# Image stores moved to ScalarE's queue, mixing weights paced on GpSimd's queue, in a Fourier layer network with a token tail

## The chip, the cores and the metric

One core of a Trainium2 chip runs the kernel. The metric is the device time of one execution in microseconds.

## What is computed

64 images of 64 x 64 pixels with 3 channels go through four Fourier layers of width 32 and a small MLP; what comes out is one value per pixel. That map of 64 rows of 64 values for each image then goes through attention, two mixture-of-experts layers and a recurrent layer. The change touches the first part alone:

```python
h = layer_norm(x @ fc0_w + fc0_b, ln0_g, ln0_b)          # (64, 64, 64, 32)
for i in range(4):
    # 12 x 12 modes at the low and high end of the spectrum, mixed over channels
    x_ft = rfft2(h);  out_ft[..., :12, :12] = einsum('bixy,ioxy->boxy', x_ft[..., :12, :12], w1[i])
    out_ft[..., -12:, :12] = einsum('bixy,ioxy->boxy', x_ft[..., -12:, :12], w2[i])
    h = irfft2(out_ft) + einsum('bchw,oc->bohw', h, conv_w[i]) + conv_b[i]
    h = layer_norm(h, ln_g[i], ln_b[i])
    if i < 3: h = gelu(h)
h = gelu(h @ fc1_w + fc1_b); h = gelu(h @ fc2_w + fc2_b); h = h @ fc3_w + fc3_b
```

All is float32. The real and imaginary parts of `w1` and `w2` are four inputs (`w1r`, `w1i`, `w2r`, `w2i`) of 4 layers x 32 x 32 x 144 values.

## The kernel before

**Groups and phases.** The 64 images are worked through in 16 groups of four. The image state h is 2 MB a group and lives in HBM (`h_scratch`); the spectrum stays on the chip. Phase `first` makes h from x and transforms it (16 groups). Phase `mid` runs three times (L = 0 to 2): for each group it transforms the mixed spectrum back (`i1` and the second half of `acc`), adds the convolution of h (`acc`), normalises, applies gelu and transforms the new h forward (`f1`, `f2`). Phase `last` does the fourth layer's inverse transform and the MLP. After it comes the token part, which the change doesn't touch.

**Bodies.** The work is software-pipelined by a string per engine (`ORDER`, from L141). A body `b` does the early steps of group b and the late ones (marked with a minus) of group b - 1. In the mid phase ScalarE's string is `gelu.2- back.1- acc.0 sq.0 gelu.3- back.2- acc.1 sq.1 back.3- acc.2 sq.2 gelu.0 acc.3 sq.3 pack.0- gelu.1 back.0 pack.1-`, and TensorE's begins `i1.0 turn.2- back.1- acc.0 i1.1`. In the first phase ScalarE has `xt.0 gelu.2- back.1- acc.0 back.2- sq.0 gelu.3- acc.1 sq.1 back.3- acc.2 sq.2 gelu.0 ...`. The number behind a step is one of four quarters of the group: `acc.n` on ScalarE (L1441) copies the product pA into `raw`, `sq` (L1451) squares it, `gelu.n` (L1462) writes quarter n of `h_new`, TensorE's `back.n` (L1318) transposes it and ScalarE's `back.n` (L1466) copies that to `h_rows`. `gelu.0` and `gelu.2` wait until the store of the group before has landed (`stored0`, `stored1`), since they overwrite it.

**Mixing.** A layer's spectrum is mixed (`mix`, L1177) in two halves of 32 images. Half 0 of the next layer is mixed ahead of the last body of a phase, half 1 between bodies 1 and 2 of the layer. The outcome y goes to HBM (`y_scratch`) by four stores of GpSimd (`y_store`, L1137), and comes back by group in eight small loads of SyncE (`load_y`, L988) into `y_in`, which `i1` reads (L1253). Groups 0 to 7 need half 0, groups 8 to 15 half 1. The weights of a layer lie in `w_sb` in two slots. VectorE centres them (`cen`, L1585 to L1589) in bodies 3 to 8 (slot 0) and 9 to 14 (slot 1); before the first of them it waits for all eight loads (`w_loaded`).

**Queues.** SyncE's queue holds, for each group g (`group`, L1067): wait for the last `i1` (or `xt`) of g, load y (or x) of g + 1, wait for `acc` 2 and load half 0 of h of g + 1, wait for `acc` 4 and load half 1, then wait for quarters 2 and 4 of `h_new` of g and store the halves. Ahead of group 2 of each mid layer it waits for the y store of half 1 (`y_is_stored`). GpSimd's queue holds the eight weight loads of layer 0 at the very start, then per layer: y store of half 0, a copy of the convolution matrix, y store of half 1, and right behind it the eight weight loads of the next layer (`weights`, L1129). At the start SyncE loads the constants, x of group 0, 16 copies of fc0's weights and its bias row (L979, L980), then 16 small tables of `gam` and `bet` (L984, L985), which `gelu.0` of group 0 waits for.

Of the kernel before, what the change touches and what calls it, by code (L numbers as in the profile page):

```python
# [33 lines left out]
LAYERS = 4  # L34
# [181 lines left out]
def build(nc, ins, out_ap, B):  # L216
    NG = B // GI
# [17 lines left out]
    with ctx:  # L235
# [77 lines left out]
        def param(rows, cols):  # L313
# [43 lines left out]
        halves = lambda t: [t[:, 0:512], t[:, 512:1024]]  # L357
        SLOTS = {"d": [pD[:]], "s": [pS[:]], "a": [pA[:]], "r": halves(pT)}
        names = ["d_full", "d_free", "s_full", "s_free", "a_full", "a_free", "r_full", "r_free", "acc_full", "conv_ready", "copied", "squared", "summed", "rooted", "root_chain",
                 "turned", "h_new_ok", "x_loaded", "y_loaded", "y_clear", "packed", "h_loaded0", "h_loaded1", "stored0", "stored1", "fc0_clear", "y_stored", "w_loaded",  # L360
                 "w_centred", "mix_a_full", "mix_a_free", "mix_b_full", "mix_b_free", "y_bias", "conv_cleared", "conv_loaded", "conv_turned", "conv_chain", "cst_loaded", "ln_loaded",
                 "fc0_loaded", "fc0_chain", "mlp_cleared", "mlp_loaded", "normed", "eps_set"]
        names += ["td_full", "td_free", "ts_full", "ts_free", "par_cleared", "par_loaded", "tok_ready", "v_chain", "shifted",
# [466 lines left out]
        def alone(eng):  # L830

            eng.sem_inc(s["passed"], 1)
# [137 lines left out]
        def _(sp):  # L970
# [29 lines left out]
                c = slice(2048 * t, 2048 * t + 2048)  # L1000
                sp.dma_start(h_in[:, c], h_dram[g][:, c]).then_inc(s[f"h_loaded{t}"], 16)

            def store_h(ph, L, g, t):
                c = slice(2048 * t, 2048 * t + 2048)
                sp.wait_ge(s["h_new_ok"], at("h_new", ph, L, g, 2 * t + 2))
                sp.dma_start(h_dram[g][:, c], h_new[:, c]).then_inc(s[f"stored{t}"], 16)

            def conv_params():
                for j in range(4):
                    sp.dma_start(conv_rows[32 * j:32 * j + 32, :].rearrange("p (l c) -> p l c", l=LAYERS),  # L1010
# [56 lines left out]
            def group(ph, L, g, then=None):  # L1067

                p = Phase(ph, L)
                end = isinstance(g, int) and g == NG - 1  # L1070
                op = "xt" if ph == "first" else "i1"
                if not (end and ph == "last"):
                    p.sent(sp, op, p.ends(op)[1], g)
                if end and ph != "last":
                    y_is_stored(L if ph == "first" else L + 1, 0)
                    load_y(0)
                    for t in range(2):
                        sp.wait_ge(s[f"stored{t}"], at("stored", ph, L, g, 0) + 16)
                        alone(sp)
                elif not end:  # L1080
                    load_x(g + 1) if ph == "first" else load_y(g + 1)
                if ph == "first" and end or ph == "mid" or ph == "last" and not end:
                    for t in range(2):
                        if ph == "last":
                            p.sent(sp, "acc", 2 * t + 1, g)
                        elif ph == "mid":
                            sp.wait_ge(s["acc_full"], at("acc", ph, L, g, 2 * t + 2))
                        load_h(0 if end else g + 1, t)
                if then:
                    then()  # L1090
                if ph != "last":
                    store_h(ph, L, g, 0)
                    store_h(ph, L, g, 1)

            def groups(ph, L):

                group(ph, L, 1)
                if ph == "mid":
                    y_is_stored(L, 1)
                else:  # L1100
                    mlp_params()
                with sp.Fori(2, NG - 1) as g:
                    group(ph, L, g)
                group(ph, L, NG - 1)

# [19 lines left out]
        def _(pool):  # L1125
            pool.memset(arena[:, 7744:8384], 0.0).then_inc(s["conv_cleared"], 1)
            pool.memset(mlp, 0.0).then_inc(s["mlp_cleared"], 1)

            def weights(L):  # L1129
                for slot in range(2):  # L1130
                    for w, (wr, wi) in enumerate((("L0_tok_w1r", "L0_tok_w1i"), ("L0_tok_w2r", "L0_tok_w2i"))):
                        for r in range(2):
                            q = slice(64 * w + 32 * r, 64 * w + 32 * r + 32)
                            pool.dma_start(w_v[q, slot].rearrange("p o m -> p (o m)"),
                                           ins[wr if slot == r else wi][L].rearrange("i o x y -> i (o x y)")).then_inc(s["w_loaded"], 16)

            def y_store(L, half):  # L1137

# [8 lines left out]
                        src = w_sb[q:q + 32, 13312:17920].rearrange("b (w n) -> b w n", w=2)  # L1147
                        pool.dma_start(dst, src).then_inc(s["y_stored"], 16)

            weights(0)  # L1150
            for L in range(LAYERS):
                y_store(L, 0)
                if L == 0:
                    pool.wait_ge(s["conv_chain"], 2)
                else:
                    pool.wait_ge(s["acc_full"], at("acc", "mid", L, 0, 0))
                pool.tensor_copy(conv_bd[:], conv_all[:, P * L:P * L + P]).then_inc(s["conv_ready"], 1)
                y_store(L, 1)
                if L < LAYERS - 1:
                    weights(L + 1)  # L1160
            pool.wait_ge(s["mix_a_full"], 6 * LAYERS)
            pool.wait_ge(s["mix_b_full"], 6 * LAYERS)
            pool.memset(spec[:, 0:at_col[0]], 0.0).then_inc(s["par_cleared"], 1)
# [242 lines left out]
        def _(act):  # L1406
# [18 lines left out]
            def steps(p):  # L1425
# [39 lines left out]
                def back(n, g):  # L1465
                    act.copy(hrow_v[:, :, 512 * n:512 * n + 512],  # L1466
                             take("back", n, g).rearrange("p (t n) -> p t n", t=2)).then_inc(s["s_free"], 1)

                def pack(b, g):

# [39 lines left out]
        def _(dve):  # L1510
# [64 lines left out]
            def cen(n, g):  # L1575
# [1 line left out]
                L, i, part = centring["L"], centring["i"], centring["part"]  # L1577
                w = w_v[:, part, :, bass.ds(24 * i, 24)]
                first = 18 * part + n
                if n == 0 and part == 0:  # L1580
                    dve.wait_ge(s["w_loaded"], 128 * L + 128)
                dve.wait_ge(s["w_centred"], 36 * L + first + 1 + 3 * i)
                alone(dve)
                if n == 0:
# [95 lines left out]
```

## Time and profile before

| what | value |
|---|---|
| median of 3 runs | 3339.99 us (3336.26 to 3341.17) |
| the profiled execution | 3339.68 us |
| its span | 3337.9 us |
| TensorE busy | 2942.9 us, 88% |
| VectorE busy | 2146.3 us, 64% |
| ScalarE busy | 1948.7 us, 58% |
| GpSimd busy | 61.5 us, 2% |
| DMA | 335.90 MB, mean 101 GB/s |
| chain that ended last, by engine | TensorE 75%, VectorE 11%, issue 5%, ScalarE 5%, DMA 4% |

The first phase runs to about 430 us, the three mid layers to about 1915, the last phase to about 2680, the token part to the end. The chain is TensorE's in the main; the 4% of DMA in it are what is left for transfers to cost. A wait of an engine is printed with what ended it, and where its entry says "issue" the profile shows nothing that it waited for.

### The profile page before, as it was taken

The numbers are of one execution on the slowest core, as the hardware profiler recorded it, in microseconds if no ns is written. First come the engines' busy times: TensorE is split into PE (matmuls) and PEld (weight loads), VectorE is DVE, ScalarE is ACT, GpSimd is POOL, SyncE is SP. The second block draws the span as 40 slices with busy tenths as digits, with TensorE's granted clock in tenths as the row PEclk, the third lists the DMA queues.
The fourth block names the chain that finished last, engine by engine and source line by source line (L and its number), as shares of the span: only waits on it lengthen the run. The fifth ranks groups of instructions, "written<-read, shape, count | busy, mean of one in ns | idle before, by whom it ended". The sixth has DMA issues, their size and how long they took to land.

```text
span 3337.9 us, 82078 instructions
## 1 busy us (share of the span) xinstructions
PE 2942.9 (88%) x32240; PEld 1869.3 (56%) x32240; DVE 2146.3 (64%) x3954; ACT 1948.7 (58%) x2271; POOL 61.5 (2%) x81
## 2 busy tenths in 40 slices
PE   5888888999888999888999879999999987973994
PEld 2454555666555666565666644444444447962893
DVE  5888676888666888666888745444544444246457
ACT  4777655666545666455666547777777763422451
POOL 0000000000000000000000010000000001000000
PEclk9999999999999999999999999999999998986897
DMA  4222346444437444447444524111111000000000
GB/s 107 99 95 98 99 161 205 163 163 162 154 135 207 162 162 162 151 144 210 163 162 162 163 75 101 55 46 44 57 54 57 29 1 1 1 1 0 1 1 13
DMA packets 98092, 335.90 MB, mean 101 GB/s; under 512 B 29928, under 2 KB 61960, under 8 KB 62088
## 3 DMA queue, kind: packets, MB, share of 16 engines
q1 hardware_dynamic: 93832, 295.73, 25.7%
q0 software_dynamic: 4096, 37.75, 4.9%
q8 instruction: 131, 2.15, 0.3%
q14 instruction: 33, 0.27, 0.0%
HBM read 179.29 MB, written 154.14 MB: 100 GB/s over the span
## 4 chain that ended last, share of the span: by engine, by line
PE 75%; DVE 11%; issue 5%; ACT 5%; DMA 4%; SPq 0%; DVEq 0%; POOL 0%; ACTq 0%; POOLq 0%
PE pA L1281 14%; PE pA L1289 7%; PE pT L1375 7%; PE pS L1318 4%; PE pT L1307 4%; PE pD L1364 4%; PE pD L1332 4%; PE pD L1346 4%; PE pD L467 3%; PE pA L467 3%; PE pA L1271 3%; PE pD L1253 2%; DMA y_in<-y_scratch 2%; PE pS L459 2%; PE pT L459 2%
## 5 line engine op out<-in xcount | busy, mean ns | idle before, releaser
L1610 DVE TENSOR_REDUCE small<-arena 128x32 f32<-128x1056 f32 x320 | 396.8, 1240 | 322.5 <-ACT arena L1451 314.0
L1281 PEld LDWEIGHTS pA<-conv_bd,h_in 128*128 128x128 f32 x4096 | 479.8, 193 | 109.4 <-issue 92.7
L1281 PE MATMUL pA<-conv_bd,h_in 128*128 128x128 f32 x4096 | 518.1, 280 | 8.6 <-DVE arena L1603 2.9
L1441 ACT COPY w_sb<-pA 128x1024 f32<-128x1024 f32 x256 | 259.7, 1015 | 417.3 <-PE pA L1289 346.4
L1624 DVE SCALAR_TENSOR_TENSOR w_sb<-w_sb,small 128x1024 f32<-128x1024 f32 x320 | 386.6, 1212 | 5.5
L1462 ACT ACTIVATE h_new<-pT,bet,gam 128x1024 f32<-128x1024 f32 x256 | 307.4, 1201 | 126.6 <-PE pT L1307 121.1
L1451 ACT ACTIVATE arena<-w_sb 128x1024 f32<-128x1024 f32 x320 | 339.2, 1060 | 13.4
L1307 PEld LDWEIGHTS pT<-cst,w_sb 128*128 128x128 f32 x2048 | 225.5, 143 | 142.8 <-issue 124.4
L1307 PE MATMUL pT<-cst,w_sb 128*128 128x128 f32 x2048 | 283.3, 282 | 21.4 <-DVE w_sb L1624 21.1
L1466 ACT COPY h_rows<-pS 128x1024 f32<-128x1024 f32 x256 | 257.0, 1004 | 72.2 <-PE pS L1318 72.1
L1318 PEld LDWEIGHTS pS<-cst,h_new 128*128 128x128 f32 x2048 | 229.4, 143 | 113.4 <-issue 72.8
L1318 PE MATMUL pS<-cst,h_new 128*128 128x128 f32 x2048 | 276.6, 279 | 9.6 <-ACT h_new L1462 9.6
L1289 PE MATMUL pA<-arena,cst 64*64 64x512 f32 x2048 | 279.1, 615 | 1.7 <-DVE arena L1603 1.7
L1375 PE MATMUL pT<-w_sb,arena 128*64 128x512 f32 x1024 | 270.3, 616 | 2.9 <-ACT w_sb L1486 1.5
L1346 PE MATMUL pD<-arena,cst 64*32 64x384 f32 (+1 forms) x4096 | 208.2, 491 | 15.0 <-DVE arena L1643 9.9
L1486 ACT ACTIVATE w_sb<-pT,arena 128x512 f32<-128x512 f32 x256 | 173.1, 685 | 18.2 <-PE pT L1375 17.4
L1643 DVE STREAM_TRANSPOSE arena<-pD 128x768 f32<-128x768 f32 x128 | 125.4, 980 | 84.6 <-PE pD L1346 68.7
L1483 ACT ACTIVATE w_sb<-pD,arena 128x1024 f32<-128x1024 f32 x128 | 142.4, 1113 | 62.1 <-PE pD L1364 38.3
L1332 PE MATMUL pD<-h_rows,cst 64*32 64x512 f32 x2048 | 139.7, 600 | 36.5 <-DVE arena L1637 21.1
L1603 DVE STREAM_TRANSPOSE arena<-pD 128x1024 f32<-128x1024 f32 x96 | 119.8, 1248 | 74.9 <-PE pD L1253 74.2
L1637 DVE STREAM_TRANSPOSE arena<-pD 128x1024 f32<-128x1024 f32 x128 | 159.2, 1244 | 5.1 <-PE pD L1332 1.1
L1271 PE MATMUL pA<-arena 128*128 128x512 f32 x256 | 126.2, 617 | 27.1 <-DVE arena L1526 24.6
(299 smaller groups left out, 3921.2 us busy)
## 6 DMA issues: line engine op xcount, KB each, us to landing
h_scratch<-h_new SPq DMA_DIRECT2D x128, 1024.0 KB, 4.2
h_in<-h_scratch SPq DMA_DIRECT2D x128, 1024.0 KB, 5.0
y_scratch<-w_sb POOLq DMA_DIRECT2D x32, 576.0 KB, 8.4
y_in<-y_scratch SPq DMA_DIRECT2D x512, 36.0 KB
w_sb<-in_L_tok_w1r_dram POOLq DMA_DIRECT2D x8, 576.0 KB, 16.6
w_sb<-in_L_tok_w1i_dram POOLq DMA_DIRECT2D x8, 576.0 KB, 16.6
w_sb<-in_L_tok_w2r_dram POOLq DMA_DIRECT2D x8, 576.0 KB, 21.0
w_sb<-in_L_tok_w2i_dram POOLq DMA_DIRECT2D x8, 576.0 KB, 21.0
```

The lines of the kernel that those rows point to most:

```text
L1281: pe.matmul(pA[:, c:c + 128], h_in[:, 1024 * n + c:1024 * n + c + 128], conv_bd[:], start=(j == 0), stop=False, skip_group_check=True)
L1289: mm = pe.matmul(pA[64 * b:64 * b + 64, 512 * t:512 * t + 512].rearrange("p (x o) -> p o x", o=C), const["idft_y"][rows, 64 * b:64 * b + 6 ...
L1307: mm = pe.transpose(bank[:, 128 * j:128 * j + 128], raw[n][:, 128 * j:128 * j + 128], ident)
L1318: mm = pe.transpose(bank[:, 128 * j:128 * j + 128], h_new[:, 1024 * n + 128 * j:1024 * n + 128 * j + 128], ident)
L1332: mm = pe.matmul(out[q:q + 32, b], const["dft_y"][rows, NQ * b:NQ * b + NQ], src[rows, t, 32 * xh:32 * xh + 32, 16 * ch:16 * ch + 16], sta ...
L1346: mm = pe.matmul(out.rearrange("p (q h c) -> p h c q", h=2, c=16), const["dft_x"][rows, 128 * part + 32 * j:128 * part + 32 * j + 32], TA[ ...
L1375: mm = pe.matmul(bank[64 * j:64 * j + 64, :], fc2_w, G1[m % 2][:, 512 * j:512 * j + 512], start=True, stop=True)
L1441: act.copy(raw[n], pA[:]).then_inc(s["copied"], 1)
L1451: act.activation(sq[n % 2][:, :, 0:C], raw[n].rearrange("p (x o) -> p x o", o=C), ACT.Square, scale=float(C) ** -0.5).then_inc(s["squared" ...
L1462: act.activation(h_new[:, 1024 * n:1024 * n + 1024], pT[:], ACT.Gelu if ph == "mid" else ACT.Identity, bias=bet[:, col], scale=gam[:, col] ...
L1610: dve.reduce_sum(var[n], sq[n % 2], axis=AX).then_inc(s["summed"], 1)
L1624: dve.scalar_tensor_tensor(out=z, in0=z, scalar=ROOT_SCALE, in1=r.broadcast_to([P, 32, C]), op0=ALU.mult, op1=ALU.mult).then_inc(s["normed ...
```

## The change

Three things. (1) `store_h` is gone from SyncE: ScalarE issues the store of a half of `h_new` itself, right behind its copies `back.1` and `back.3`. (2) SyncE's wait for the y store of half 1 moves from ahead of group 2 to ahead of group 6; in the first phase the loads of the MLP's parameters move with it. (3) GpSimd issues the weights in pairs (`weights(L, slot, w)`), each behind a wait for a certain `acc` product: at the start in bodies 0, 1, 3 and 4; in a layer the first pair right behind the mix, the second behind `acc.1` of body 2, the y store of half 1 behind `acc.0` of body 4, and the pairs of slot 1 behind `acc.0` of bodies 5 and 6. VectorE waits per slot (`w_loaded0`, `w_loaded1`), with one more semaphore increment (`alone`) at each first step of the centring.

```diff
-            def store_h(ph, L, g, t):
-                c = slice(2048 * t, 2048 * t + 2048)
-                sp.wait_ge(s["h_new_ok"], at("h_new", ph, L, g, 2 * t + 2))
-                sp.dma_start(h_dram[g][:, c], h_new[:, c]).then_inc(s[f"stored{t}"], 16)
-
...
                 if then:
                     then()
-                if ph != "last":
-                    store_h(ph, L, g, 0)
-                    store_h(ph, L, g, 1)
 
             def groups(ph, L):
 
-                group(ph, L, 1)
+                with sp.Fori(1, 6) as g:
+                    group(ph, L, g)
                 if ph == "mid":
                     y_is_stored(L, 1)
                 else:
                     mlp_params()
-                with sp.Fori(2, NG - 1) as g:
+                with sp.Fori(6, NG - 1) as g:
                     group(ph, L, g)
                 group(ph, L, NG - 1)
...
+            def weights(L, slot, w):
+                wr, wi = (("L0_tok_w1r", "L0_tok_w1i"), ("L0_tok_w2r", "L0_tok_w2i"))[w]
+                for r in range(2):
+                    q = slice(64 * w + 32 * r, 64 * w + 32 * r + 32)
+                    pool.dma_start(w_v[q, slot].rearrange("p o m -> p (o m)"),
+                                   ins[wr if slot == r else wi][L].rearrange("i o x y -> i (o x y)")).then_inc(s[f"w_loaded{slot}"], 16)
+
+            def after(ph, L, g, n):
+
+                pool.wait_ge(s["acc_full"], at("acc", ph, L, g, n))
...
-            weights(0)
+            for slot in range(2):
+                for w in range(2):
+                    after("first", 0, 3 * slot + w, 1)
+                    weights(0, slot, w)
...
-                y_store(L, 1)
-                if L < LAYERS - 1:
-                    weights(L + 1)
+                if L == LAYERS - 1:
+                    y_store(L, 1)
+                else:
+                    n = 2 * L + 1
+                    pool.wait_ge(s["mix_a_free"], 3 * n + 3)
+                    pool.wait_ge(s["mix_b_free"], 3 * n + 3)
+                    weights(L + 1, 0, 0)
+                    after("mid", L, 2, 2)
+                    weights(L + 1, 0, 1)
+                    after("mid", L, 4, 1)
+                    y_store(L, 1)
+                    for w in range(2):
+                        after("mid", L, 5 + w, 1)
+                        weights(L + 1, 1, w)
...
                 def back(n, g):
                     act.copy(hrow_v[:, :, 512 * n:512 * n + 512],
                              take("back", n, g).rearrange("p (t n) -> p t n", t=2)).then_inc(s["s_free"], 1)
+                    if n % 2:
+                        c = slice(1024 * n - 1024, 1024 * n + 1024)
+                        act.dma_start(h_dram[g][:, c], h_new[:, c]).then_inc(s[f"stored{n // 2}"], 16)
...
-                if n == 0 and part == 0:
-                    dve.wait_ge(s["w_loaded"], 128 * L + 128)
+                if n == 0:
+                    dve.wait_ge(s[f"w_loaded{part}"], 64 * L + 64)
+                    alone(dve)
```

## Rows read from the trace of the kernel before

**Rows 1.** The waits of all engines: engine, line, tile, releaser: us in total, times, longest.
```profile
PE pD L1253 <- DMA y_in<-y_scratch: 27.1, 3, 10.7
```

**Rows 2.** The timeline, 0 to 60: start, us, engine, line, operation, idle time before.
```profile
10.87 0.25 SPq L980 DMA_DIRECT2D arena<-in_L_tok_fc_b_dram  x1
...
14.80 5.53 SPq L984 DMA_DIRECT2D gam<-in_L_tok_ln_g_dram  x1
...
28.87 0.42 DVE L1522 COPY arena<-arena 1x512 f32<-1x512 f32 x1 [23.10 <-DMA arena<-in_L_tok_fc_b_dram]
...
44.58 1.19 ACT L1462 ACTIVATE h_new<-pT,bet,gam 128x1024 f32<-128x1024 f32 x1
```

**Rows 3.** DMA issues by line: tile, count, size of each, median us to landing.
```profile
arena<-in_L_tok_fc_b_dram SPq DMA_DIRECT2D x2, 0.2 KB, 2.3
```

**Rows 4.** The timeline, 490 to 550: end of a mix and body 2 of L = 0.
```profile
505.23 0.50 POOL L1134 DMA_DIRECT2D w_sb<-in_L_tok_w1r_dram  x1
...
506.13 1.00 ACT L1466 COPY h_rows<-pS 128x1024 f32<-128x1024 f32 x1
...
508.47 0.91 PE L1253 MATMUL pD<-y_in,cst 48*32 48x208 f32 x32
...
514.15 1.01 ACT L1441 COPY w_sb<-pA 128x1024 f32<-128x1024 f32 x1 [1.44 <-PE pA L1289]
...
516.71 4.11 SPq L996 DMA_DIRECT2D y_in<-y_scratch  x8
...
520.55 1.21 ACT L1462 ACTIVATE h_new<-pT,bet,gam 128x1024 f32<-128x1024 f32 x1
...
541.41 1.59 PE L1253 MATMUL pD<-y_in,cst 48*32 48x208 f32 x32 [10.12 <-DMA y_in<-y_scratch]
...
546.94 1.45 DVE L1585 TENSOR_REDUCE small<-w_sb 128x24 f32 x1
```

**Rows 5.** Windows: us, busy PE, PEld, DVE, ACT, POOL, then clock, DMA share, GB/s.
```profile
531.30:541.40 10.10, 0.00 (x0) 0.02 (x1) 1.14 (x2) 1.34 (x2) 0.00 (x0) 0.64 1.01 221
```

**Rows 6.** TensorE's timeline from 560: `i1` of bodies 3 and 4, and two gaps.
```profile
572.12 0.91 PE L1253 MATMUL pD<-y_in,cst 48*32 48x208 f32 x32 [0.29 <-DVE arena L1643]
...
1026.87 1.57 PE L1346 MATMUL pD<-arena,cst 64*32 64x384 f32 x23 [1.30 <-issue]
...
1040.19 1.59 PE L1253 MATMUL pD<-y_in,cst 48*32 48x208 f32 x32 [10.72 <-DMA y_in<-y_scratch]
...
1070.68 0.91 PE L1253 MATMUL pD<-y_in,cst 48*32 48x208 f32 x32 [0.29 <-DVE arena L1643]
...
1098.33 0.91 PE L1253 MATMUL pD<-y_in,cst 48*32 48x208 f32 x32 [0.29 <-DVE arena L1643]
...
1528.35 0.85 PE L1346 MATMUL pD<-arena,cst 64*32 64x384 f32 x1 [3.60 <-issue]
...
1537.36 1.59 PE L1253 MATMUL pD<-y_in,cst 48*32 48x208 f32 x32 [6.26 <-DMA y_in<-y_scratch]
...
1566.77 0.91 PE L1253 MATMUL pD<-y_in,cst 48*32 48x208 f32 x32 [0.29 <-DVE arena L1643]
```

**Rows 7.** Line 1006, SyncE's stores of h_new: duration of the issue, and landing.
```profile
L1006 SPq DMA_DIRECT2D h_scratch<-h_new x128: 332/355/372, 49.8 to 1928.1; - x128
...
DMA to landing us min/median/max: 3.9/4.2/21.5
```

**Rows 8.** ScalarE's timeline, 560 to 590: a mid body.
```profile
577.80 1.02 ACT L1441 COPY w_sb<-pA 128x1024 f32<-128x1024 f32 x1 [1.35 <-PE pA L1289]
...
587.55 1.01 ACT L1441 COPY w_sb<-pA 128x1024 f32<-128x1024 f32 x1 [1.20 <-PE pA L1289]
```

**Rows 9.** ScalarE's timeline, 200 to 248: a body of the first phase.
```profile
223.58 1.01 ACT L1441 COPY w_sb<-pA 128x1024 f32<-128x1024 f32 x1 [0.32 <-PE pA L1271]
...
233.01 1.20 ACT L1462 ACTIVATE h_new<-pT,bet,gam 128x1024 f32<-128x1024 f32 x1 [0.36 <-PE pT L1307]
```

**Rows 10.** Line 1134, GpSimd's weight loads: landing.
```profile
DMA to landing us min/median/max: 7.3/20.7/35.7
```

More of the change, by code:

```diff
@@ L359, in build @@
         names = ["d_full", "d_free", "s_full", "s_free", "a_full", "a_free", "r_full", "r_free", "acc_full", "conv_ready", "copied", "squared", "summed", "rooted", "root_chain",
-                 "turned", "h_new_ok", "x_loaded", "y_loaded", "y_clear", "packed", "h_loaded0", "h_loaded1", "stored0", "stored1", "fc0_clear", "y_stored", "w_loaded",
+                 "turned", "h_new_ok", "x_loaded", "y_loaded", "y_clear", "packed", "h_loaded0", "h_loaded1", "stored0", "stored1", "fc0_clear", "y_stored", "w_loaded0", "w_loaded1",
                  "w_centred", "mix_a_full", "mix_a_free", "mix_b_full", "mix_b_free", "y_bias", "conv_cleared", "conv_loaded", "conv_turned", "conv_chain", "cst_loaded", "ln_loaded",
@@ L1127, in _ @@
             pool.memset(mlp, 0.0).then_inc(s["mlp_cleared"], 1)
[L1129 to L1135, printed above, removed]
+            def weights(L, slot, w):
[6 more added lines that the diff above has]
+                pool.wait_ge(s["acc_full"], at("acc", ph, L, g, n))
             def y_store(L, half):
```

## The prediction

> **What bounds the kernel now.** I read the waits first, sorted by total: they say which engine is stopped by a transfer, which is all that this change can touch. Of everything that TensorE waits for, one entry names a DMA: its L1253 (the inverse x transform, `i1`) waited 27.1 us in three goes for `y_in` [rows 1]. Then the timeline of the start. VectorE's copy of the fc0 bias row (L1522) starts at 28.87 after 23.10 us of idling for a load that SyncE had issued at 10.87 [rows 2]; a load of that size lands in 2.3 us elsewhere [rows 3]. What stands in its way are the eight mixing weight loads (576 KB each) that GpSimd issues in the first microseconds.
>
> Then the timeline of one layer (L = 0). The mix of half 1 is over at about 503. GpSimd stores y, and from 505.23 on issues the eight weight loads of the next layer [rows 4]. SyncE may load the y of group 3 only when that store has landed, so it issues it at 516.71 to 520.82, behind the weights, and it is in place at 541.4, 20.6 us later. TensorE has nothing from 531.3 on and starts at 541.41; in that gap its granted clock falls to 0.64 while the DMA engines are 1.01 busy [rows 4, 5]. In the other bodies of a layer TensorE goes from one `i1` to the next in 27.65 us (1070.68 to 1098.33) [rows 6] with waits of a few tenths; nothing there hangs on a DMA. So the gain, if any, lies at the start and once per layer, and the loss, if any, in the 60-odd ordinary bodies where ScalarE now issues stores.
>
> **The change part by part, against the profiled 3339.7 us (its span is 3337.9; the median of the runs, 3340.0, is the same number for my purpose).**
>
> *1. Start.* GpSimd's first weights now wait for the first `acc` product, which itself needs fc0. So nothing large is in flight when the fc0 row is issued at 10.87 (0.25 us). With 2.3 us to landing it is there at 13.4 [rows 3] instead of 28.87: 15.4 us earlier. All work after it moves with it, TensorE's slow first products too, since it idles before them either way. What is late next: `gelu.0`, at 44.58 [rows 2], would be at 29.2, and it needs the 16 small `gam`/`bet` loads that SyncE issues behind fc0. Without congestion these take 0.43 us each, and are issued by 18.7; one of them took 5.53 behind the weights [rows 2]. I take this as covered: **-15.4**, with 5 as the lower end if those loads are slow by themselves (issued by 27.5 as now, then landing at 39 instead of 29).
>
> *2. y of group 3.* The wait of SyncE for the half 1 store moves from ahead of group 2 to ahead of group 6, where the loads of group 7 on follow; the first group that reads half 1 is 8, so nothing reads too early. The store itself moves to the first `acc` of body 4 and has until body 6, over 40 us. The load of group 3's y now follows `i1.1` of body 2 (508.47 + 0.91 = 509.4), and its eight issues end near 514: 17.5 us ahead of its use at 531.3. It was 20.6 us from the last issue with eight weights, four y stores and four h transfers around it. Now half of the weights and no y stores are in that body. I take the wait as gone: **-27.1** [rows 1]. With the old 20.6 us, 3.1 us a layer would stay.
>
> *3. The body after the stall.* It starts at the low clock: 32 matmuls of `i1` take 1.59 us after the gap and 0.91 otherwise [rows 4, 6], and 1.59/0.91 is about the step between 2.4 and 1.2 GHz. Bodies 3 of the three layers take 30.71 (541.41 to 572.12), 30.49 and 29.41 us against 27.65 [rows 4, 6]: together 7.7 us over. With no gap this goes: **-7.7**.
>
> *4. Gaps put down to issue in body 2.* 1.30 us at 1026.87 and 3.60 us at 1528.35 [rows 6]: in the middle of a product, waiting for nothing, as if the engine's code came late. Such gaps are absent in the looped bodies. If the full DMA engines hold the code back they vanish (-4.9), if not, they stay (0). Half: **-2.5**.
>
> *5. Stores on ScalarE.* Two issues a body, 120-odd in all. On SyncE one takes 0.355 us, 0.372 at most, at any load of the DMA engines [rows 7], plus under 0.1 us for its address; no row shows a DMA issued by ScalarE. I take 0.45. Below it could be 0 (issue beside the running copy), above it GpSimd's 0.50 [rows 4] + 0.1. Behind `back.1` in the mid bodies ScalarE idles 1.35 us before `acc.0`, behind `back.3` 1.20 before `acc.2` [rows 8]: covered at either end, 0. In the first phase the idle time before `acc.0` is 0.32 [rows 9]; so `acc.0`, `sq.0`, `gelu.3` come 0.15 later, TensorE's `back.3` with them. Behind `back.3` there is next to nothing, but `gelu.0` has idled 0.36 before it [rows 9]. That leaves 0.1 to 0.3 a body, in 15 bodies at most 4.5: **+2**.
>
> *6. Where the stores are late.* `gelu.0` may overwrite `h_new` only when the store of half 0 has landed. Before, that was issued in the previous body. Now it is issued behind `back.1`: in body 2 after 507.1, ahead of `gelu.0` at 520.55 [rows 4], 13.4 us; in the first phase 223.7 to 233.0, 9.3 us [rows 9]. Landing is 4.2 us by the median, 21.5 at most [rows 7], and the long ones belong to the weight bursts. In bodies 1, 3 and 4 of the first phase two weight loads now start beside that store. Sharing the engines evenly doubles 4.2 to 8.4: just covered. **+1**, up to 9 (3 us in three bodies).
>
> *7. Weights in time?* The centring (`cen.0`, L1585) of body 3 stands 5.5 us behind its `i1` (546.94 against 541.41) [rows 4], so at 536.8 without the stall. It needs all four loads of slot 0; the last two are issued after `acc.1`, whose copy begins at 514.15 [rows 4], so by 515.2: 21.6 us. Landing took 7.3 / 20.7 / 35.7 us (least, median, most) with eight in flight [rows 10]. With two in flight I place it near the lower end. Slot 1 has bodies. By the longest landing VectorE would stand 14.1 us in each layer: bounds 0 and +42, taken **0**. The Trainium skill (DMA: Bandwidth & Descriptors, Anatomy of one DMA — SWDGE (gpsimd) path) gives such a transfer as about 2.0 us + bytes / 436e3, which is 3.4 us for one and under 7 for two. By that estimate this wait cannot occur; the rows, where the least is 7.3, are slower than it, and what stands above goes by them. The added `alone` and waits of VectorE at `cen` are 48 times under 0.05 us, **+0.5** in all counting that this engine is nearly full in the first phase.
>
> Sum: -15.4 - 27.1 - 7.7 - 2.5 + 2 + 1 + 0.5 = -49.2; 3339.7 - 49.2 = **3290 us**.
>
> **The rivals.**
> - *y still late.* y's small packets stand in SyncE's queue beside two others, ScalarE's stores and GpSimd's weights. For: DMA engines stay nearly full in body 2 (2.4 MB weights, 4.2 MB of h, 0.3 of y in 27.65 us are 248 GB/s, and 221 is what 1.01 gave [rows 5]). Against: the first two weights have 6 us of lead and are mostly in. Price: 3.1 us a layer, half of term 3 back (3.9) and term 4 (2.5): +15.7, 3306. The Trainium skill (DMA: Bandwidth & Descriptors, Queues, rings and completion order) says that each DMA engine takes turns between queues packet by packet; by that rule a third queue costs y a share of its turns, in the direction of this rival.
> - *The centring waits.* Landing of 27 us, between the median and the most of [rows 10], where 21.6 are free, gives 5.4 us of VectorE in three layers, +16 and 4 of clock: 3310.
> - *The start is bound by the small loads.* Term 1 is 5 instead of 15.4: 3300.
> - *ScalarE's issue is dear*, the one on the slower side. It sits ahead of `acc.0` and `acc.2` of every body. With c us per issue including its address, a mid body loses (c - 1.35) + (c - 1.20), a first body about (c - 0.68) + (c - 0.44). Over 48 and 15 bodies this is 50 us at c = 1.5: from there the change is a loss. At c = 1.8 it is 50 + 37 = 87 us: 3290 - 2 + 87 = 3375. For it: SyncE's one issue of 5.53 [rows 2] shows that an issue can block, and no row shows ScalarE's. Against: 128 large stores never took over 0.372 us [rows 7], even with full engines.
> - *It does not do what it says.* If the weights' bursts only move to other bodies and stall TensorE there, the 27.1 come back: bodies 5 and 6 get four loads together, where the stores' slack is 13.4 us and the y loads' 17. I hold this small: at most 20 us, 3310.
>
> **How the numbers follow.** The forecast has 0.68, with its own range of 3280 to 3300 (terms 4 and 5 at their ends, terms 6 and 7 partly). Late y 0.10, centring 0.06, small loads at the start 0.08, moved bursts 0.03, dear issue 0.05. The range of 8 in 10 is **3276 to 3314**: from all of term 4 and a free ScalarE issue, with some more of the clock, to the late y and centring cases together with first-phase store waits. A measurement of this kernel tells 0.2% (6.7 us) from no change. Faster by more than that: 0.94 (all cases but dear issue, less a little); within it: 0.02; slower: 0.04.
>
> **What the profile after would show.** Right: L1522 starts near 13 us; no wait of L1253 for `y_in`; bodies 2 and 3 of each layer at 27.65 to 29 us; ScalarE's issues at 0.3 to 0.5 us with mid bodies still at 27.65 and first bodies at most 0.3 longer; L1585 of body 3 not waiting for a weight load. Wrong: `gelu.0` or `gelu.2` (L1462) waiting for `h_scratch<-h_new`, above all in bodies 1, 3 and 4 of the first phase; L1585 or L1462 of group 0 waiting for a DMA; longer mid bodies. The prediction falls as a whole if ordinary bodies change by over half a microsecond, for there are 60 of them.

## The result, and the profile after

The changed kernel takes 3281.86 us (median of 4, 3278.74 to 3284.09) against 3338.55 beside it: ratio 0.983, 95% interval 0.981 to 0.985, 56.7 us faster. Forecast were 3290 and 49.2 us. Two of the nine executions of run 4 were far slower than the rest (3490 and 3808 us), and its time and ratio below leave them out. The profiled execution has a span of 3279.2 us, 58.7 less than before. Its page, the lines on busy time, the slices and the DMA queues, and from part 4 the chain by engine:

```profile
PE 2937.9 (90%) x32240; PEld 1867.7 (57%) x32240; DVE 2145.9 (65%) x3954; ACT 1950.3 (59%) x2271; POOL 61.9 (2%) x81
...
q1 hardware_dynamic: 75400, 161.50, 16.4%
q10 hardware_dynamic: 18432, 134.23, 10.0%
q0 software_dynamic: 4096, 37.75, 5.3%
...
PE 79%; DVE 11%; issue 5%; ACT 5%; DVEq 0%; SPq 0%; DMA 0%; ACTq 0%
```

The engines do the same work. ScalarE's stores are a queue of their own now (q10, 134 MB, what was taken off q1), and the DMA's part of the chain went from 4% to 0. The wait of TensorE for `y_in` [rows 1] is gone from the list of waits. The start, as in [rows 2] (timeline of all engines):

```profile
12.10 0.42 DVE L1535 COPY arena<-arena 1x512 f32<-1x512 f32 x1 [6.33 <-DMA arena<-in_L_tok_fc_b_dram]
...
14.07 3.75 PE L1281 MATMUL pA<-arena 128*128 128x512 f32 x4 [7.79 <-DVE arena L1539]
...
18.07 0.42 SPq L985 DMA_DIRECT2D bet<-in_L_tok_ln_b_dram  x1
18.13 0.67 POOL L1126 DMA_DIRECT2D w_sb<-in_L_tok_w1r_dram  x1 [16.49 <-PE pA L1281]
...
18.92 1.98 PE L1281 MATMUL pA<-arena 128*128 128x512 f32 x4 [1.10 <-ACT w_sb L1451]
```

The copy of the fc0 row starts 16.8 us earlier than in [rows 2], and all small tables are issued by 18.5 without one that blocks. Body 2 of L = 0 and the `i1` of bodies 3 and 4, as in [rows 4, 6] (TensorE's timeline; `i1` is L1263 here):

```profile
485.60 1.57 PE L1263 MATMUL pD<-y_in,cst 48*32 48x208 f32 x32 [1.24 <-ACT w_sb L1432]
...
513.26 1.58 PE L1356 MATMUL pD<-arena,cst 64*32 64x384 f32 x23 [0.48 <-issue]
...
516.01 0.91 PE L1263 MATMUL pD<-y_in,cst 48*32 48x208 f32 x32 [0.16 <-DVE arena L1657]
...
543.66 0.91 PE L1263 MATMUL pD<-y_in,cst 48*32 48x208 f32 x32 [0.29 <-DVE arena L1657]
```

In this layer body 2 begins at a low clock, behind the mix with its gaps on TensorE, as the stretches of the trace show (columns: stretch and its length; busy time and instructions of PE, PEld, DVE, ACT and POOL; granted clock; DMA share; GB/s):

```profile
485.60:489.00 3.40, 3.40 (x41) 2.75 (x42) 1.70 (x4) 0.00 (x0) 1.00 (x2) 0.52 0.74 173
489.90:492.00 2.10, 2.10 (x22) 1.93 (x24) 1.22 (x1) 1.44 (x2) 0.00 (x0) 1.00 1.00 202
```

A granted clock of 0.52 is near the 1.2 GHz level, and 1.00 follows within some 4 us. It is not so in every layer or execution: over its first 3.5 us body 2 has 1.00 in L = 1 and 0.59 in L = 2 of this trace, and 1.00 in L = 0 of a second one of the same kernel (run 9). The kernel before has 1.00, 1.00 and 0.54. There a low clock also came behind the late y, where now body 3 begins with a gap of 0.16 us and takes 0.91 us for its first product instead of 1.59:

```profile
541.40:543.00 1.60, 1.59 (x33) 0.81 (x34) 0.00 (x0) 0.00 (x0) 0.00 (x0) 0.50 0.98 385
```

(the kernel before, the same view, over that first product of body 3). Body 3 now lasts 27.65 us. GpSimd's part of bodies 2 to 4, then SyncE's, in their timelines:

```profile
485.80 0.50 POOL L1126 DMA_DIRECT2D w_sb<-in_L_tok_w1r_dram  x1 [95.60 <-ACT w_sb L1432]
...
498.70 0.49 POOL L1126 DMA_DIRECT2D w_sb<-in_L_tok_w2r_dram  x1 [11.90 <-PE pA L1299]
...
549.61 2.10 POOL L1144 DMA_DIRECT2D y_scratch<-w_sb  x4 [49.93 <-PE pA L1299]
```
```profile
493.94 4.23 SPq L996 DMA_DIRECT2D y_in<-y_scratch  x8
498.58 11.17 SPq L1001 DMA_DIRECT2D h_in<-h_scratch  x2
...
550.38 14.37 SPq L996 DMA_DIRECT2D y_in<-y_scratch  x8
```

In body 4, beside the four y stores of GpSimd, the eight y issues of SyncE take 14.4 us in place of 4.2 (14.0 and 14.4 in the other layers). Nothing waits for them: body 4 lasts 27.64 us.

And line 1480, ScalarE's stores, then line 1126, the weights, as in [rows 7, 10]:

```profile
L1480 ACTq DMA_DIRECT2D h_scratch<-h_new x128: 338/343/387, 34.4 to 1871.9; - x128
...
  ACT h_new L1472: 2.7, 1
...
DMA to landing us min/median/max: 3.9/4.5/14.1
```
```profile
DMA to landing us min/median/max: 5.4/7.7/11.2
```

The weights land in 7.7 us by the median where it was 20.7, and no store takes over 14.1 where it was 21.5.

Where the 58.7 us are, read from the starts of `xt` and `i1` in TensorE's timeline, before against after:

| stretch | before, us | after, us | difference |
|---|---|---|---|
| up to the `xt` of body 1 | 48.77 | 30.58 | -18.2 |
| from there to the first `i1` of L = 0 | 380.64 | 381.54 | +0.9 |
| bodies 2 of the three layers | 38.49 + 40.19 + 40.50 | 30.41 + 27.68 + 29.23 | -31.9 |
| bodies 3 of the three layers | 30.71 + 30.49 + 29.41 | 27.65 + 27.64 + 27.64 | -7.7 |
| all the rest | | | -1.8 |

The ordinary bodies of the layers are the same to 0.01 us (27.64), and twelve bodies of the first phase take 289.47 against 289.36. The figures of body 2 hold a part that changes between executions: the low clock at its start and gaps put down to issue are worth up to 3 us (30.41 and 27.51 us, both in L = 0 of the changed kernel).

### The profile page after: what moved, and what is told of

It reads as the page before. It is cut to its first block, busy times and chain, and to the rows that moved or that the text cites. A ratio compares the mean times of both kernels' runs of the same rounds, so it can differ in the third digit from the quotient of the medians.

```text
span 3279.2 us, 82177 instructions
## 1 busy us (share of the span) xinstructions
PE 2937.9 (90%) x32240; PEld 1867.7 (57%) x32240; DVE 2145.9 (65%) x3954; ACT 1950.3 (59%) x2271; POOL 61.9 (2%) x81
## 4 chain that ended last, share of the span: by engine, by line
PE 79%; DVE 11%; issue 5%; ACT 5%; DVEq 0%; SPq 0%; DMA 0%; ACTq 0%
PE pA L1291 15%; PE pA L1299 8%; PE pT L1385 8%; PE pT L1317 5%; PE pS L1328 5%; PE pD L1342 4%; PE pD L1374 4%; PE pD L1356 4%; PE pD L467 3%; PE pA L467 3%; PE pD L1263 3%; PE pA L1281 3%; PE pS L459 2%; PE pT L459 2%; DVE arena L1657 2%
## 5 line engine op out<-in xcount | busy, mean ns | idle before, releaser
L1499 ACT ACTIVATE w_sb<-pT,arena 128x512 f32<-128x512 f32 x256 | 173.1, 685 | 16.5 <-PE pT L1385 15.4
L1374 PE MATMUL pD<-h_new,arena 32*128 32x512 f32 x512 | 145.5, 644 | 3.6 <-issue 1.7
```

Source lines behind the costliest of these rows:

```text
L1374: mm = pe.matmul(out, fc1_w[rows, :], h_new[rows, 512 * u:512 * u + 512], start=True, stop=True)
```

## The experiments

The theory (A): two bursts of weight loads and what they hold up are the whole gain, and the queue of the stores is worth nothing. Rival B: it is the queues, loads alone on SyncE's; or the misplaced wait alone.

**1. Stores back on SyncE.** The changed kernel with this edit (and `store_h` as it was), and `back`'s issue on ScalarE removed:

```diff
...
+                if ph != "last":
+                    store_h(ph, L, g, 0)
+                    store_h(ph, L, g, 1)
```

> The changed kernel with its stores back on SyncE's queue, behind the loads of the same group; pacing and the moved wait stay. Theory A (the gain is the two weight bursts and the misplaced wait, the stores' queue is worth nothing): SyncE loads the y of group 3 only after it has stored quarter 4 of group 1, some 2 to 3 us later than in the changed kernel, still over 10 us before its use, so 3282 us, within 3 us of the changed kernel. Rival B (loads alone on SyncE's queue are what brings y in time): TensorE waits for y again, 5 to 10 us in each of three layers, 3297 to 3312 us.

Measured: 3285.48 us, ratio 0.984 (0.982 to 0.985) to the kernel before. No wait for `y_in`, and the intervals of this and the changed kernel overlap in most of their length. The bodies 2 take 27.52, 31.59 and 27.62 us; the long one begins at a granted clock of 0.50 and has no wait of 0.5 us or more. A holds: the stores' queue is not what the gain comes from. Its time is 3.6 us above the changed kernel's median, a little beyond A's 3 us, which these few executions do not resolve.

**2. Stores on ScalarE, nothing else.** The kernel before with

```diff
-                if ph != "last":
-                    store_h(ph, L, g, 0)
-                    store_h(ph, L, g, 1)
...
+                    if n % 2:
+                        c = slice(1024 * n - 1024, 1024 * n + 1024)
+                        act.dma_start(h_dram[g][:, c], h_new[:, c]).then_inc(s[f"stored{n // 2}"], 16)
```

> The kernel before with only its stores moved to ScalarE's queue. Theory A: SyncE's wait for the y store of half 1 still holds the y load back and the weights are in its way, so the three waits of TensorE for y stay near 27 us in total: 3336 to 3342 us, no change. Rival B: the y load lands earlier by what SyncE no longer waits, 5 us a layer or more: 3323 us or less. Rival C (a ScalarE issue costs its engine): 3341 to 3350 us.

Measured: 3347.17 us, ratio 1.0023 (1.0014 to 1.0033): slower by 7.5 us, outside A's 3336 to 3342. Its waits:

```profile
PE pD L1245 <- DMA y_in<-y_scratch: 46.2, 3, 16.1
```

46.2 us for y in place of 27.1. Its SyncE and TensorE timelines:

```profile
521.23 3.80 SPq L996 DMA_DIRECT2D y_in<-y_scratch  x8
```
```profile
547.06 1.59 PE L1245 MATMUL pD<-y_in,cst 48*32 48x208 f32 x32 [15.21 <-DMA y_in<-y_scratch]
```

y is issued 17.0 us into body 2 (which begins at 504.23), in the kernel before 13.8 [rows 4]. The four y stores that it waits for landed in 9.6 us by the median and 14.8 at most, where the kernel before has 8.5 and 11.6; an h store was in flight beside them. Then y took 22.0 us from its last issue to its use, 20.6 before (22.1 and 21.7 in the other two layers, 22.3 and 22.5 before, so only the first step is clearly longer). ScalarE itself lost nothing: its mid bodies are at 27.64. So neither A ("no change") nor C ("an issue costs ScalarE") had it right. The move of the stores costs something: y comes later within the burst.

**3. The burst back at the start.** The changed kernel with

```diff
             for slot in range(2):
                 for w in range(2):
-                    after("first", 0, 3 * slot + w, 1)
                     weights(0, slot, w)
```

> The changed kernel with all eight weight loads of layer 0 issued at the very start again. Theory A: the copy of the fc0 row starts near 29 us again, and the whole kernel is later by the 18 us that the trace of the changed kernel gained before body 1: 3299 to 3301 us. Rival (the start was bound by SyncE's small loads, and the gain came from elsewhere): 3282 to 3290 us.

Measured: 3301.85 us (ratio 0.989, 0.988 to 0.991), 20.0 above the changed kernel. `xt` of body 1 starts at 48.35, as before (48.77). The start is worth 18 to 20 us. The bodies of the first phase and of the layers are as in the changed kernel, apart from the clock at the start of body 2 (27.53, 30.03 and 29.25 us).

**4. The burst back in the layers.** The changed kernel with the y store and all eight loads right behind the mix:

```diff
-                if L == LAYERS - 1:
-                    y_store(L, 1)
-                else:
-                    n = 2 * L + 1
-                    pool.wait_ge(s["mix_a_free"], 3 * n + 3)
-                    pool.wait_ge(s["mix_b_free"], 3 * n + 3)
-                    weights(L + 1, 0, 0)
-                    after("mid", L, 2, 2)
-                    weights(L + 1, 0, 1)
-                    after("mid", L, 4, 1)
-                    y_store(L, 1)
-                    for w in range(2):
-                        after("mid", L, 5 + w, 1)
-                        weights(L + 1, 1, w)
+                y_store(L, 1)
+                if L < LAYERS - 1:
+                    for slot in range(2):
+                        for w in range(2):
+                            weights(L + 1, slot, w)
```

> The changed kernel with the y store of half 1 and all eight weight loads issued in one burst right behind the mix, as before; the moved wait, the stores on ScalarE and the paced start stay. If the misplaced wait alone held y back, the y load issued 7 us earlier than before lands in time: 3282 to 3286 us. Theory A (bandwidth taken by the burst matters as well): y lands some 3 to 8 us late in each layer, or the stores (17 us to landing within a burst, 13.4 free) hold gelu.0 up by 4 us; with the low clock behind each stall 3295 to 3315 us.

Measured: 3332.45 us (ratio 0.998, 0.997 to 0.999), 50.6 above the changed kernel and far beyond A's 3315. Its waits, then SyncE's timeline and TensorE's:

```profile
PE pD L1254 <- DMA y_in<-y_scratch: 35.1, 3, 14.0
ACT h_new L1463 <- DMA h_scratch<-h_new: 11.3, 5, 4.8
```
```profile
496.68 8.22 SPq L996 DMA_DIRECT2D y_in<-y_scratch  x8
```
```profile
529.40 1.59 PE L1254 MATMUL pD<-y_in,cst 48*32 48x208 f32 x32 [10.00 <-DMA y_in<-y_scratch]
```

y is issued 9.6 us into body 2 (it begins at 487.10), 4 us earlier than before, its eight issues take 8.2 us instead of 4.1, and it is used 24.5 us after the last of them (26.5 and 24.9 in the other layers). The run to compare is run 2, which has the same burst and the same queue for the stores. There y is issued 17 us into body 2 and used 42.8, 43.0 and 43.5 us into it; here it is issued 7 to 10 us into body 2 and used 42.3, 43.2 and 42.5 us into it. Issued early or late, y arrives when the burst is nearly through. Of its weights only the last load is still out then; it lands 33.1 to 35.7 us after its issue in the kernel before and 41.8 to 42.5 here, 0.6 to 5.9 us after y is used. `gelu.0` waits for the store of h too, by 4.1 and 4.8 us in two of the layers.

**5. The wait alone.** The kernel before with `y_is_stored` moved to ahead of group 6:

```diff
-                group(ph, L, 1)
+                with sp.Fori(1, 6) as g:
+                    group(ph, L, g)
...
-                with sp.Fori(2, NG - 1) as g:
+                with sp.Fori(6, NG - 1) as g:
```

> The kernel before with only SyncE's wait for the y store of half 1 moved from ahead of group 2 to ahead of group 6; bursts and SyncE's stores stay. Theory A (the burst of weights decides when y lands): the y load is issued some 4 us earlier, amid the burst, and lands when the burst ends; TensorE still waits 20 us or more for y in three layers: 3330 to 3342 us. Rival (the wait was the cause): no wait for y, 3300 to 3310 us.

Measured: 3340.44 us, ratio 1.000 (0.999 to 1.001). Its list of waits has

```profile
PE pD L1254 <- DMA y_in<-y_scratch: 29.1, 3, 11.1
```

As A has it: y is issued 0.8 us earlier in L = 0 and 3.8 in the other layers, counted from the start of body 2, and is used 38.3, 40.0 and 38.4 us into it, against 38.5, 40.2 and 40.5. Moving this wait, by itself, brings nothing that the time shows.

**6. The pairs without the moved wait.** The changed kernel with y store and wait where they were (stores on ScalarE and paced start stay):

```diff
-                with sp.Fori(1, 6) as g:
-                    group(ph, L, g)
+                group(ph, L, 1)
...
-                with sp.Fori(6, NG - 1) as g:
+                with sp.Fori(2, NG - 1) as g:
...
+                    y_store(L, 1)
                     weights(L + 1, 0, 0)
                     after("mid", L, 2, 2)
                     weights(L + 1, 0, 1)
-                    after("mid", L, 4, 1)
-                    y_store(L, 1)
```

> The changed kernel, but with the y store of half 1 right behind the mix and SyncE's wait for it ahead of group 2, as before; only the weights are in pairs. Theory A: y is issued 13 us into body 2 as before, but two loads in place of eight are beside it, so it lands well before its use: no wait for y, 3280 to 3288 us. Rival (wait and pacing are both needed): TensorE waits 3 to 8 us a layer, 3295 to 3310 us.

Measured: 3296.28 us (ratio 0.987, 0.986 to 0.989), 14.4 above the changed kernel. The time is the rival's, the mechanism mostly another:

```profile
ACT h_new L1470 <- DMA h_scratch<-h_new: 15.8, 5, 5.5
...
PE pD L1261 <- DMA y_in<-y_scratch: 4.6, 1, 4.6
```

y is late once. What is late in the layers is the landing of h's store, behind y store and weights: `gelu.0` of body 2 waits 5.50 us in L = 0 and 4.34 in L = 1. The bodies 2 are 31.5 to 32.0 us where the changed kernel has 27.7 to 30.4. Bodies 2 and 3 together are 11.0 us above the changed kernel's, of the 39.6 that they gained. So pacing the weights gives some three quarters of the gain in the layers, and putting the y store off, with the wait that allows it, about the rest. That share is an estimate: two of these bodies 2 begin at the low clock (first `i1` 1.57 and 1.59 us), in the changed kernel one does so in full. Another 3.0 us of this run lie ahead of body 1, which the edit does not touch: three of its first products are slow.

**7. Each store in four.** The changed kernel with

```diff
-                        c = slice(1024 * n - 1024, 1024 * n + 1024)
-                        act.dma_start(h_dram[g][:, c], h_new[:, c]).then_inc(s[f"stored{n // 2}"], 16)
+                        for k in range(4):
+                            c = slice(1024 * n - 1024 + 512 * k, 1024 * n - 512 + 512 * k)
+                            act.dma_start(h_dram[g][:, c], h_new[:, c]).then_inc(s[f"stored{n // 2}"], 16)
```

> The changed kernel with each store of ScalarE cut into four of 256 KB: 8 issues a body in place of 2, about 1.7 us of issuing in each of the two places, same bytes. Theory A (ScalarE's sequencer issues while its datapath runs, so only what exceeds the gap to the next product counts): mid bodies stay at 27.65 us, first bodies gain at most 0.3 us: 3282 to 3290 us. Rival (an issue takes its place in ScalarE's time as a copy does): (1.7 - 1.35) + (1.7 - 1.2) us in 48 bodies and 2.3 us in 15, 74 us: 3350 us or more.

Measured: 3320.70 us (ratio 0.995, 0.993 to 0.996), 38.8 above the changed kernel, between the two. ScalarE's timeline in a mid body, and the stores' line:

```profile
615.11 0.34 ACTq L1482 DMA_DIRECT2D h_scratch<-h_new  x1
615.46 1.00 ACT L1476 COPY h_rows<-pS 128x1024 f32<-128x1024 f32 x1
615.63 1.36 ACTq L1482 DMA_DIRECT2D h_scratch<-h_new  x3
617.80 1.01 ACT L1451 COPY w_sb<-pA 128x1024 f32<-128x1024 f32 x1 [1.35 <-PE pA L1299]
```
```profile
L1482 ACTq DMA_DIRECT2D h_scratch<-h_new x512: 338/352/3217, 34.4 to 1913.7; - x171
```

1.7 us of issuing run beside the copy, which starts 0.35 us after the first issue; the copy of `acc.0` has the same 1.35 us of idle time before it as with one issue, and ordinary mid bodies stay at 27.64. In the first phase a body grows by 0.37 us (293.94 in place of 289.47 for twelve). That is A's picture. What A missed are the bodies with other large transfers. Those with the y store of half 1 grow from 27.64 to 31.43, 31.74 and 31.71 us, the last ones of L = 1 and 2, with that of half 0, from 29.2 and 27.7 to 35.3 and 35.4, and one issue takes up to 3.2 us. There the issue itself blocks, and ScalarE with it. Its timeline in the last body of L = 1:

```profile
1375.88 7.70 ACTq L1482 DMA_DIRECT2D h_scratch<-h_new  x4
1383.98 1.01 ACT L1451 COPY w_sb<-pA 128x1024 f32<-128x1024 f32 x1 [7.10 <-issue]
```

Four issues take 7.7 us (8.0 in L = 2), and the copy of `acc.0` stands behind them for 7.1 us. I have not separated whether the number of transfers or of their rows does it.

**8. The second pair late.** `after("mid", L, 2, 2)` became `after("mid", L, 2, 4)`.

> The changed kernel with the second pair of weights of slot 0 behind acc.3 of body 2 in place of acc.1, so 11 us ahead of the centring that needs them in place of 22. With landings as in the changed kernel (5.4 to 11.2 us) VectorE does not wait, or by under 1 us: 3280 to 3286 us. If the landing with the next body's transfers beside it is nearer to 20 us, as in the burst, VectorE and with it TensorE stand 5 to 9 us in each layer: 3300 to 3310 us.

Measured: 3280.91 us (ratio 0.983, 0.981 to 0.984), the changed kernel's time. But VectorE does wait for the second pair, 2.47, 0.70 and 0.89 us at the first centring of the three layers:

```profile
520.13 1.48 DVE L1599 TENSOR_REDUCE small<-w_sb 128x24 f32 x1 [2.47 <-DMA w_sb<-in_L_tok_w2i_dram]
```

That is over the 1 us that I allowed, and far under the rival's 5 to 9. The bodies 3 take 28.96, 28.46 and 27.65 us for 27.64, and what of this the wait costs is not settled, since in the first of them TensorE also has a gap of 0.81 us put down to issue. The last load of the pair is issued 9.7 to 9.9 us ahead of where the centring would start, and the longest landing of a weight load is 11.6 us. The 22 us of the changed kernel cover that with 10 to spare.

**9. Both pairs at once**, and the changed kernel again beside it. The edit takes `after("mid", L, 2, 2)` out.

> The changed kernel itself, unchanged, as the yardstick for the two beside it: 3279 to 3285 us.

> The changed kernel with both pairs of slot 0 issued together right behind the mix (four loads, 2.4 MB); y store and slot 1 stay deferred. Theory A (what hurts is transfers waiting behind more than the body can move; four loads are 12 us of DMA at the 200 GB/s of the bursts): they are in before the store of half 0 is due at 13 us behind its issue; no wait, 3279 to 3288 us. Rival (any weights in a lump delay y and the stores as the eight did): gelu.0 waits 3 us or more in each layer, 3291 us or more.

Measured: the changed kernel 3278.85 us (ratio 0.982, 0.980 to 0.983), with both pairs at once 3286.44 (0.983, 0.982 to 0.985). The intervals of the ratios overlap, but the five executions (3283.1 to 3287.0) lie above seven of the nine of the changed kernel (3277.6 to 3285.3), so this variant may be a few us slower. The four loads, by the DMA issues of the window 484 to 500:

```profile
w_sb<-in_L_tok_w1r_dram POOLq DMA_DIRECT2D x1, 576.0 KB, 5.5
w_sb<-in_L_tok_w1i_dram POOLq DMA_DIRECT2D x1, 576.0 KB, 7.9
w_sb<-in_L_tok_w2r_dram POOLq DMA_DIRECT2D x1, 576.0 KB, 10.9
w_sb<-in_L_tok_w2i_dram POOLq DMA_DIRECT2D x1, 576.0 KB, 12.9
```

They are issued 0.5 us apart and land 2.5 to 3.5 us one behind another, the last in 12.9 us, and the store beside them in 11.3, just within its 13. In bodies 2 and 3 nothing waits for a DMA, as A has it (body 0 of L = 0 has one wait of 0.7 us for h): bodies 2 take 30.56, 27.53 and 27.63 us, the yardstick's 27.51, 27.97 and 29.22. Most of what the two profiles differ by lies elsewhere. Of the 8.8 us between the two spans 1.5 are before body 1 and 1.6 in body 2 of the first phase, which this edit does not touch; 1.0 is in the bodies 2 of the layers. So four loads are bearable, eight with four stores of y are not.

**10. A faster start.** The changed kernel with `T2` cleared first on VectorE and

```diff
-            for x in range(16):
+            for x in range(0, 16, 2):
                 sp.dma_start(fc0[3 * x:3 * x + 3, x, :], ins["L0_tok_fc0_w"]).then_inc(s["fc0_loaded"], 16)
...
+            act.wait_ge(s["fc0_chain"], 1)
+            for x in range(1, 16, 2):
+                act.dma_start(fc0[3 * x:3 * x + 3, x, :], ins["L0_tok_fc0_w"]).then_inc(s["fc0_loaded"], 16)
```

(with the bias row on ScalarE too).

> The changed kernel with VectorE clearing fc0's block first (before pD, sq and y_in) and half of the 17 fc0 loads issued by ScalarE. With the start bound by the chain clear, 17 issues, landing: the block is cleared 2.2 us earlier and 9 issues at 0.31 us stand in place of 17, so the fc0 copy starts near 7.8 instead of 12.1 us and the kernel is 4 to 5 us faster than the changed one: 3275 to 3281 us. If the landing or the low clock of the first products sets the start instead: no difference.

Measured: 3276.28 us (0.982, 0.980 to 0.984), 2.6 below the yardstick, which the intervals do not tell apart. Its timeline:

```profile
8.06 0.42 DVE L1538 COPY arena<-arena 1x512 f32<-1x512 f32 x1 [2.18 <-DMA arena<-in_L_tok_fc_b_dram]
...
10.03 3.75 PE L1280 MATMUL pA<-arena 128*128 128x512 f32 x4 [3.70 <-DVE arena L1542]
...
14.88 3.61 PE L1280 MATMUL pA<-arena 128*128 128x512 f32 x4 [1.10 <-ACT w_sb L1454]
```

The copy is 4.0 us earlier, as expected, but `xt` of body 1 only 2.8 (27.80 against 30.58). The second product takes 3.61 us for its four matmuls where the changed kernel's took 1.98. The granted clock is 1.00 in the record in both, so the record does not show what slows it. My alternative was a low clock of the first products; no low clock is on record, but a slow second product took a third of the gain.

## Why the prediction was right

**Start, term 1 (-15.4; measured -18.2 in the trace, 20.0 by run 3).** The mechanism holds. Two sizes were off. The fc0 row landed 1.0 us after its issue and not 2.3: the row I took (2.3 us for 0.2 KB) [rows 3] was of a load that stood beside others. And the second `acc` product took 1.98 us for 3.76, which gave 1.8 more; the granted clock is 1.00 in both kernels' records of it. This second part is luck: of the nine profiles of kernels with a paced start four have a slow second product (3.56 to 3.78 us). The small loads that I feared behind `gelu.0` landed in 1.7 to 2.0 us and never blocked: without the burst none of their issues takes over 0.43 us, so the 5.53 of [rows 2] went with it.

**y, terms 2 and 4 (-27.1 and -2.5, together -29.6; measured -31.9 over the bodies 2).** Size right, within the 3 us by which one body 2 differs between two executions. The place of the issue was right too: y is issued 6.7 to 8.3 us into body 2, forecast were 6.5. But the text gave the gain to two things side by side, the earlier issue and the lighter body, as if each brought a part, and it expected the old 20.6 us of landing to cost 3.1 us a layer. Run 5 shows that the earlier place alone brings nothing and run 4, beside run 2, that it brings nothing within a burst: y lands when the burst is nearly through. Run 6 shows the reverse, that y is nearly in time without the earlier place, and that it is the store of h which is late. The gaps at issue within L1346's product (1.30 us in L = 1, 3.60 in L = 2) are gone in those two layers of the changed kernel's trace, but L = 0 has 0.48 us, and its second trace has 1.11 in L = 2. Such gaps come and go without a full burst beside them too, so these runs do not show that the DMA engines cause them.

**The body after, term 3 (-7.7; measured -7.7).** 30.71, 30.49 and 29.41 us became 27.65, 27.64 and 27.64.

**ScalarE's issues, term 5 (+2; measured +0.1).** An issue takes 0.34 us, as on SyncE. It doesn't stand behind the copy but beside it. In the changed kernel's timeline of ScalarE in the first phase:

```profile
204.33 0.34 ACTq L1480 DMA_DIRECT2D h_scratch<-h_new  x1
204.59 1.00 ACT L1476 COPY h_rows<-pS 128x1024 f32<-128x1024 f32 x1
205.91 1.01 ACT L1451 COPY w_sb<-pA 128x1024 f32<-128x1024 f32 x1 [0.32 <-PE pA L1281]
```

The idle 0.32 us before `acc.0` are those of [rows 9]. The step that failed is to have charged the issue to the time between two copies; my lower end, 0, was the truth. For the same reason the dear issue rival, decided at 1.5 us by my sum, was wrong in its working: run 7 issued 1.7 us in each place and ordinary mid bodies lost nothing, where that working takes 0.85 us from each. Its row, an issue that blocks, was the real danger: it takes congestion.

**Stores landing late, term 6 (+1; measured +0.9 for the whole first phase).** One wait of 2.67 us for the store, but in none of the bodies 1, 3 and 4 that I named. ScalarE's timeline of the changed kernel:

```profile
405.03 1.21 ACT L1472 ACTIVATE h_new<-pT,bet,gam 128x1024 f32<-128x1024 f32 x1 [2.67 <-DMA h_scratch<-h_new]
```

It is in the last body of the phase, where the four y stores of half 0 are beside it. Four y stores weigh twice what a pair of weights does, and I had looked only for what the change moves. The 0.9 us hold the 0.1 of term 5, and 0.5 of them are in body 1.

**Weights in time, term 7 (0; measured 0).** 11.2 us at most against 21.6 free; run 8 shows that some 10 free are not quite enough. The Trainium skill's estimate (DMA: Bandwidth & Descriptors, Anatomy of one DMA — SWDGE (gpsimd) path) of 3.4 us for one such load is under the trace's least, 5.4 us; the measurement decides, and here both leave room.

**The sum.** 3290 is 8 us above the measured 3281.9, and by spans the gain is 9.5 us larger than forecast: 2.8 from the start, 2.3 from the bodies 2, 2.6 from ScalarE's issues, late stores and `alone`, which were charged 3.5 and took 0.9, and 1.8 from the rest, which I have not placed. The terms that miss do so to the same side, none by more than 3 us, so the total is off by more than any of them.

**The rivals.** Late y came true in runs 2, 4 and 5, in each of them beside the full burst, and in one layer of run 6 (4.6 us), beside y store and one pair. The bursts did not move their harm to other bodies: bodies 4 to 6, where y store and slot 1 now are, stay at 27.64 or 27.65 us. The Trainium skill's rule that each DMA engine takes turns between queues (DMA: Bandwidth & Descriptors, Queues, rings and completion order) has the sign of run 2, where with a third queue the longest landing of a y store was 3.2 us later and y itself, in L = 0, another 1.4; no run here shows the turns themselves.

What stays open: bodies outside the loops vary between executions of the same code (body 2 of L = 0: 30.41 and 27.51 us in two profiles of the changed kernel), by the granted clock at their start (0.52 and 1.00 over the first 3.5 us) and by gaps put down to issue. They make up most of the 3.8 us between those two spans. The low clock comes behind the mix in kernels with and without the burst, and what decides when is open. Nor do the runs tell whether the stores on ScalarE bring anything in the paced kernel (3285.5 against 3281.9 and 3278.9).

## What to carry over

In this kernel the transfer that TensorE waited for was late by what was in flight with it, whatever the queue of the stores and, within the burst, whenever it was issued. So first spread the large loads that nobody needs soon, then look at order. Check each transfer of the stretch that is left: the next one to be late may be a store whose buffer is wanted again. A DMA issue on ScalarE was free here in ordinary bodies; beside other large transfers four smaller ones stopped the engine for up to 7.1 us.

## What was not expected of the hardware

- ScalarE issues a DMA while its copies run: 1.7 us of issues beside a copy of 1.0 us cost a mid body nothing (27.64 us).
- A blocked issue: up to 3.2 us for one on ScalarE (256 KB stores, run 7) and up to 2.9 for one on SyncE. Eight small ones on SyncE take 8.2 us beside run 4's burst and 14.4 beside the y stores of the changed kernel, 4.1 to 4.2 otherwise.
- Eight small loads of y, 0.3 MB together, are used 20.6 to 26.5 us behind their last issue beside 4.7 MB of weights (runs 2, 4, 5 and the kernel before).
- The first products take nearly twice their time, for one, two or three products (four matmuls in 3.5 to 3.8 us, then 1.98; three in run 6), in kernels whose start is the same up to there. The record has a granted clock of 1.00 over them:

```profile
14.00:17.90 3.90, 3.75 (x4) 1.17 (x4) 0.00 (x0) 0.04 (x1) 0.00 (x0) 1.00 0.10 1
```

This is the changed kernel's first product; what slows it, no run here shows.
